# Splitting all first expert weights in the key turns of the walk, two halves a turn, and adding the last skip rows tile by tile

## The reference

```python
xn = _layernorm(x)
# graph attention, summed over the edges of each target node
e = leaky_relu(el[src] + er[dst]); ex = exp(e - emax[dst])
rst = segment_sum(feat[src] * (ex / denom[dst]), dst)
x = x + (xn + elu(rst + bias)) + linear_attention(xn)
# experts: W1 is (8, 256, 1024), W2 is (8, 1024, 256)
h = gelu((layernorm(x) * ln_g + ln_b) @ W1[e] + b1[e])
x = x + sum over the two chosen experts of weight * (h @ W2[e] + b2[e])
```

## Time and profile before

| | us |
|---|---|
| median of 3 runs | 1894.84 (1893.95 to 1897.71) |
| profiled execution, its own time | 1891.82 |
| its span, first to last instruction | 1890.1 |
| start of the walk's first add and end of its last | 119.3 and 1198.4 |
| busy: PE, DVE, POOL, ACT | 1581.7, 1368.5, 1218.3, 1079.1 |
| mean granted TensorE clock | 0.937 of full speed |

### The profile page before, as it was taken

How to read it: one execution, slowest core, us unless ns; L and a number is a source line. 1 busy time by engine, 2 the same in 40 slices (tenths; PEclk the granted TensorE clock), 3 DMA queues, 4 the chain that set the end, 5 groups by cost and what they waited for, 6 DMA issues and landing times. The chain is left out here.

```text
span 1890.1 us, 46784 instructions
## 1 busy us (share of the span) xinstructions
PE 1581.7 (84%) x11358; PEld 1300.0 (69%) x11358; DVE 1368.5 (72%) x3833; ACT 1079.1 (57%) x3043; POOL 1218.3 (64%) x1135
## 2 busy tenths in 40 slices
PE   7858777788787989888887778629999999999995
PEld 5635555455566777777775666517888889888884
DVE  6656567677667888888888999897666656665662
ACT  4655566566666666677666776563444444444441
POOL 2077777777777777777677776105666666666663
PEclk8978899999999999999998888658999999999998
DMA  7745565566544555555555665652333333333332
GB/s 223 247 122 138 168 174 164 165 176 179 150 117 127 155 150 150 141 152 145 142 139 179 183 202 162 200 199 45 53 48 53 49 48 50 53 50 49 46 53 24
DMA packets 149158, 239.37 MB, mean 127 GB/s; under 512 B 27536, under 2 KB 114824, under 8 KB 147624
## 3 DMA queue, kind: packets, MB, share of 16 engines
q0 software_dynamic: 61216, 132.39, 30.4%
q1 hardware_dynamic: 85944, 103.15, 16.8%
q10 hardware_dynamic: 1744, 0.85, 0.2%
HBM read 180.78 MB, written 55.52 MB: 125 GB/s over the span
## 5 line engine op out<-in xcount | busy, mean ns | idle before, releaser
L843 POOL DMA_INDIRECT w_s<-table,w_s x784 | 806.4, 1029 | 279.9 <-issue 231.4
L2092 PE MATMUL bank<-w_s 128*128 128x260 f32 x1952 | 515.9, 410 | 110.3 <-DVE w_s L1536 110.0
L2092 PEld LDWEIGHTS bank<-w_s 128*128 128x128 f32 x1952 | 378.1, 201 | 206.0 <-DVE w_s L1536 139.9
L1026 ACT ACTIVATE w_s<-w_s 128x64 f32 x976 | 260.3, 337 | 68.3 <-ACT w_s L1021 68.1
L1536 DVE SCALAR_TENSOR_TENSOR w_s<-w_s 128x256 f32<-128x256 f32 x732 | 275.7, 426 | 26.7 <-ACT w_s L1026 18.9
L2294 PE MATMUL bank<-acc,w_s 128*128 128x256 f16 (+1 forms) x2736 | 290.4, 265 | 1.6 <-DVE acc L1937 1.5
L2315 PE MATMUL bank<-w_s,acc 128*128 x2520 | 284.5, 273 | 7.2 <-DVE acc L1951 5.5
L907 POOL DMA_INDIRECT out<-mid_g,low_g x105 | 177.2, 1687 | 151.2 <-ACT mid_g L1197 90.6
L2294 PEld LDWEIGHTS bank<-acc,w_s 128*128 x2736 | 252.9, 98 | 30.7 <-issue 2.1
L2315 PEld LDWEIGHTS bank<-w_s,acc 128*128 128x128 f16 x2520 | 245.8, 98 | 37.0 <-issue 8.7
L1033 ACT COPY w_s<-bank 128x512 bf16<-128x512 bf16 x244 | 142.1, 582 | 202.8 <-PE bank L2072 202.3
(11 more groups left out here) (308 smaller groups left out, 2187.6 us busy)
## 6 DMA issues: line engine op xcount, KB each, us to landing
stage<-in_L_ffn_W SPq DMA_DIRECT2D x32, 512.0 KB, 4.2
w_s<-table,w_s POOLq DMA_INDIRECT x784
w_s<-in_x SPq DMA_DIRECT2D x48, 256.0 KB, 4.0
w_s<-xT_d SPq DMA_DIRECT2D x96, 128.0 KB
w_park<-low_g SPq DMA_DIRECT2D x18, 512.0 KB
w_s<-w_park SPq DMA_DIRECT2D x9, 1024.0 KB, 9.1
xn_d<-acc SPq DMA_DIRECT2D x7, 896.0 KB, 5.0
table<-w_s SPq DMA_DIRECT2D x24, 260.0 KB, 3.5
```

What stands on the lines that cost most here:

```text
L843: pool.indirect_dma_start(out=ring[:, u, k, :], out_offset=None, in_=table[:, :], in_offset=bass.IndirectOffsetOnAxis(ap=srcT[:, (q * RING ...
L1026: last = act.activation(m[:, e, 0:GD], rows[:, e, 0:GD], ACT.Copy, scale=m[:, e, GD:HC])
L2092: last = pe.matmul(bank[2 + k.at % 2][:, 0:ROW], hot32[:, k.at % 4, s, :], msg[:, k.at % 2, s, :], start=s == 0, stop=s == SUB - 1)
```

## The change

- All 32 halves, W1's too, are split and parked in the key turns. `PARKS` goes from 18 halves to 16 pairs of halves; the pairs are handled in turns 2 to 17, two halves a turn. Each half has its own space: `stage[:, u]`, and as the place of the result `low_g` for u = 0 and `mid_g` for u = 1. ACT splits the first after step 1 of a turn and the second after step 2, DVE one step later each, as one piece of 1024 columns instead of two of 512. SP no longer waits for a store to land before it issues the next load; ACT waits for it before it overwrites the space.
- The split turns are gone: `SPLIT_TURNS`, `act_split1`, `dve_split1` and SP's W1 loads there. Turns 52 to 60 have no hook, and the late work stays at its steps. SP loads the parked W1 of experts 0 to 4 after the late work of groups 0 to 4, experts 5 and 6 right after the walk and ahead of the W2 loads there, expert 7 as before.
- The load of the first skip rows is now ahead of any weights.
- POOL adds the skip rows of groups 5 and 6 in seven instructions of one tile (256 columns) each instead of one of 1792.

```diff
-PARKS = 2 * (X + 1)
+PARKS = 2 * X
...
+        park_s = [whole[:, :, :].rearrange("p a b -> p (a b)")[:, 0:FF].bitcast(F16).rearrange("p (h f) -> p h f", h=2)
+                  for whole in (low_g, mid_g)]
...
-            def store_half(h):
-                sp.wait_ge(park_low, h + 1)
-                sp.dma_start(w_park[h // 2, :, h % 2], park_s[:, :, :]).then_inc(park_out, 16)
-                sp.wait_ge(park_out, (h + 1) * 16)
+            def store_half(e, u):
+                sp.wait_ge(park_low[u], e + 1)
+                sp.dma_start(w_park[e, :, u], park_s[u][:, :, :]).then_inc(park_out[u], 16)
...
-                h = t // 2 - 3
-                if t % 2 == 0 and 0 <= h < PARKS:
-                    store_half(h)
-                    if h + 1 < PARKS:
-                        load_half(h + 1)
+                e = t // 2 - 3
+                if t % 2 == 0 and 0 <= e < PARKS:
+                    for u in range(2):
+                        store_half(e, u)
+                        if e + 1 < PARKS:
+                            load_half(e + 1, u)
...
+            def load_w1(e):
+                sp.dma_start(w1_s[:, e, :, :, :], w_park[X + e]).then_inc(w1_in, 16)
...
+            load_mid(0)
             for u in range(2):
-                load_w1(0, u)
-            load_mid(0)
-            group_added(0)
-            next_w1(1)
-            next_w1(2)
...
+                sp.wait_ge(park_out[u], 16 * PARKS)
...
+            for g in range(5):
+                group_added(g)
+                load_w1(g)
             sp.wait_ge(msg_ready, J)
             load_mid(GROUPS - 1)
             sp.wait_ge(acc_done, J)
+            load_w1(5)
+            load_w1(6)
             load_w2(1)
...
             def add_mid(g):
-                z = acc[:, g * RG:(g + 1) * RG, 0:D]
...
-                pool.tensor_tensor(z, z, mid_of(g)[:, :, :], ALU.add).then_inc(x2_made, 1)
+                for k in range(RG):
+                    z = acc[:, g * RG + k, 0:D]
+                    last = pool.tensor_tensor(z, z, mid_of(g)[:, k, :], ALU.add)
+                last.then_inc(x2_made, 1)
...
             def park_hook(b, u):
                 keys_hook(b, u)
-                if u == 1:
-                    act.wait_ge(park_in, (b - 1) * 16)
-                    act.activation(park_s[:, 0, :], stage[:, 0, :], ACT.Copy, scale=WSCALE).then_inc(park_high, 1)
+                if u in (1, 2):
+                    e, half = b - 2, u - 1
+                    act.wait_ge(park_in[half], (e + 1) * 16)
+                    if e:
+                        act.wait_ge(park_out[half], e * 16)
+                    act.activation(park_s[half][:, 0, :], stage[:, half, :], ACT.Copy, scale=WSCALE).then_inc(park_high[half], 1)
...
-            def dve_split1(n, u):
...
+            def dve_park(e, half):
+                dve.wait_ge(park_high[half], e + 1)
+                dve.scalar_tensor_tensor(park_s[half][:, 1, :], stage[:, half, :], WSCALE, park_s[half][:, 0, :],
+                                         ALU.mult, ALU.subtract).then_inc(park_low[half], 1)
```

More of the change, by code:

```diff
@@ L123, in past, with walk_turns @@
         return not isinstance(self.n, int) or self.n >= least
-def walk_turns(eng, slot, keys, park, queries, split, end_slot=None, late=None):
+def walk_turns(eng, slot, keys, park, queries, end_slot=None, late=None):
     def turn(b, beside, c):
@@ L145, in walk_turns @@
         turn(q0 + c, queries, c)
-    for n in range(SPLIT_TURNS):
-        turn(s0 + n, split, n)
-    for b in range(s0 + SPLIT_TURNS, end):
+    for b in range(q0 + QUERY_TURNS, end):
         turn(b, None, b)
@@ L508, in build @@
         blank_turn = sem("blank_turn")
-        park_in, park_high, park_low, park_out = sem("park_in"), sem("park_high"), sem("park_low"), sem("park_out")
+        park_in, park_high, park_low, park_out = (
+            [sem(f"{name}{u}") for u in range(2)] for name in ("park_in", "park_high", "park_low", "park_out"))
         w1_in, w2_in, b2_in = sem("w1_in"), sem("w2_in"), sem("b2_in")
-        stage_in = [sem(f"stage_in{u}") for u in range(2)]
-        high_ready = [sem(f"high_ready{u}") for u in range(2)]
-        low_ready = [sem(f"low_ready{u}") for u in range(2)]
         den_turn, scaled, z_exp, elu_made, x2_made = (
@@ L696, in _ @@
                 sp_chunk(c)
-            def load_w1(n, u):
-                sp.dma_start(stage[:, u, :], w1[bass.ds(n, 1), u * P:(u + 1) * P, :].rearrange("e p f -> p (e f)")).then_inc(stage_in[u], 16)
+            def load_w1(e):
+                sp.dma_start(w1_s[:, e, :, :, :], w_park[X + e]).then_inc(w1_in, 16)
             def load_mid(g):
@@ L724, in store_xn2 @@
                              acc[:, g * RG:(g + 1) * RG, 0:D]).then_inc(xn2_out[g % 2], 16)
-            def next_w1(n):
-                for u in range(2):
-                    sp.wait_ge(low_ready[u], n)
-                    load_w1(n, u)
             def group_added(g):
@@ L735, in group_added @@
                 store_x2(g)
+            load_mid(0)
             for u in range(2):
-                load_w1(0, u)
-            load_mid(0)
-            group_added(0)
-            next_w1(1)
-            next_w1(2)
-            group_added(1)
-            next_w1(3)
-            group_added(2)
-            next_w1(4)
-            next_w1(5)
-            group_added(3)
-            next_w1(6)
-            for u in range(2):
-                sp.wait_ge(low_ready[u], X - 1)
+                sp.wait_ge(park_out[u], 16 * PARKS)
             sp.dma_start(b2_b, b2.rearrange("(a e) d -> a e d", a=1).to_broadcast([P, X, D])).then_inc(b2_in, 16)
-            group_added(4)
+            sp.wait_ge(mid_out, 16 * (PAIRS + 1))
+            for g in range(5):
+                group_added(g)
+                load_w1(g)
             sp.wait_ge(msg_ready, J)
@@ L1625, in dve_mid @@
                 last.then_inc(mid_ready, 1)
-            def dve_split1(n, u):
-                dve.wait_ge(high_ready[u], n + 1)
-                dve.scalar_tensor_tensor(w1_half(n, u, 1), stage[:, u, :], WSCALE, w1_half(n, u, 0),
-                                         ALU.mult, ALU.subtract).then_inc(low_ready[u], 1)
-            def dve_park(b, k):
-                dve.wait_ge(park_high, b - 1)
-                half = slice(k * (FF // 2), (k + 1) * (FF // 2))
-                last = dve.scalar_tensor_tensor(park_s[:, 1, half], stage[:, 0, half], WSCALE, park_s[:, 0, half],
-                                                ALU.mult, ALU.subtract)
-                if k == 1:
-                    last.then_inc(park_low, 1)
+            def dve_park(e, half):
+                dve.wait_ge(park_high[half], e + 1)
+                dve.scalar_tensor_tensor(park_s[half][:, 1, :], stage[:, half, :], WSCALE, park_s[half][:, 0, :],
+                                         ALU.mult, ALU.subtract).then_inc(park_low[half], 1)
             def park_hook(b, u):
@@ L1642, in park_hook @@
                 if u >= 2:
[L1643 removed]
+                    dve_park(b - 2, u - 2)
             def keys_hook(b, u):
@@ L2337, in _ @@
             pe_turn_rows(0)
-            for u in range(2):
-                pe.wait_ge(low_ready[u], X - 1)
-            pe.wait_ge(w1_in, 16)
+            pe.wait_ge(w1_in, 16 * X)
             for s in range(FT):
```

34 lines of the change are left out of this document (11 added, 23 removed).

## The result

The changed kernel takes 1902.04 us (median of 7 runs, 1896.06 to 1906.53); the kernel before, beside it, 1896.15 (7 runs, 1893.95 to 1897.71). The ratio is 1.0034, with a 95% interval of 1.0019 to 1.0049: **slower by about 6 us**, where the prediction said 17 us faster.

A forecast was written before the change was run, and what follows sets the result against it. POOL's gathers bound the key turns, DVE the split turns. Terms +3.5 - 13.4 - 3.3 - 2.8 - 1.0 = -17.0 us took the profiled 1891.8 to 1874.8, expected median 1878; 8-in-10 range 1869 to 1890.

The forecast's parts named there:

- What bounds each stage: Key turns 2 to 17: POOL's gathers set the pace; split turns 52 to 58: DVE, busy 125.6 of 130.3 us.
- SP's queue in the key turns: Turns 2 to 17: doubled stores and loads, 54 GB/s on top of 165, cost nothing, hidden by POOL's pace.
- The rival: Key turns: transfers come in one burst, POOL finds rows late; 24 us over 16 turns, 1902 in all; chance 0.06.
- The gathers beside the splits: Turns 2 to 17: DVE splits of 14 more halves lengthen POOL's gathers, +3.5 us (+2.9 to +5.2).
- The rival's 14.4 us: Key turns: splits block gathers for their whole length, costing 14.4 instead of 3.5 us, 1889 in all; chance 0.10.
- The split turns: -13.4: Turns 52 to 58: 17.1 us of DVE splits removed, 3.7 given back as idle time; bounds -15.4 and -5.7.
- The first skip rows: Turn 51: DVE's 4.12 us wait for `mid_g` shrinks as that load goes first, -3.3 us; bounds -2 and -4.1.
- The tile-by-tile adds: Walk's end: DVE waits for one piece of POOL's add at most, -2.8 us; at the second add, -1.0.
- After the walk: Behind the walk: two more parked megabytes, 6.4 us at 330 GB/s, delay nothing wanted before a gap ends; 0.

The follow-up runs named there:

- the splits small: Changed kernel with the splits of every half after the first expert's cut from 1024 to 64 columns, all transfers at full size: 1893.92 us (one run).
- small transfers: Changed kernel with every half after the first expert's cut to 128 columns a row in its loads and stores, splits whole: 1890.05 us (one run).
- both small: Changed kernel with every half after the first expert's cut to 128 columns a row in its transfers and 64 columns in its splits: 1872.73 us (one run).
- staggered halves with two DVE pieces each: Changed kernel with a turn's two halves taken half a turn apart and DVE's split in two 512-column pieces in separate slots: 1877.59 us, ratio 0.9908.

## Why the prediction was wrong

- *What bounds each stage* was right: POOL in the key turns, DVE in the split turns.
- *SP's queue in the key turns: "I price this at nothing; what hides it is the same POOL pace."* **This is the step that failed.** POOL's pace hides nothing from POOL itself, which waits for the rows of its own earlier gathers. I added 54 GB/s to 165 and compared averages, where the change put four transfers of 0.5 MB into 2.5 us and took out the wait that had spaced them. POOL idles 23.2 us more beyond its ordinary gaps, 14.4 of it in waits that the profile names. With the splits small the burst costs 25.1 us; in the changed kernel spacing the same transfers gives back 14.6 to 16.9. The rival had the mechanism and, in part by luck, the price (24 us, 1902): it took one wait of 1.49 us from another stage for every turn, where the long waits were 0.9 to 3.1 us. I gave it a chance of 0.06, because I took the longest wait of before, 0.3 us, for its likelihood, though the pacing behind it was being removed.
- *The gathers beside the splits: +3.5.* Too low as a price of the splits, though the gathers of the changed kernel took only 5.0 us more. In a steady stream it is 17.3 us (small transfers against both small) with two long pieces a turn. I divided the average over all gathers by the number of halves, "near the lower end, since the instructions become one instead of two a half". That is the wrong way round: a piece of 0.68 us caught a gather's start 12 times in 32, one of 1.21 us 31 times in 32, and with more left (0.63 us instead of 0.50). The average without splits that I subtracted was no base either, since message pieces and hit matrices hold gathers up in those turns too. The rule of the Trainium skill that I weighed against the average holds for every gather that starts in a split. The rival's 14.4 us comes near the 14.8 counted by coincidence: it is the growth of DVE's busy time on splits, while the time lost to them grew by 11.1 (4.5 to 15.6), 5.8 of which the other DVE instructions gave back.
- *The split turns: -13.4.* -10.6 in the changed kernel, DVE busy 109.7 (108.5 foretold) and idle 10.0 of 119.7 us, 1.4 a turn instead of 1.2. In the other kernels of the changed form the same turns give -11.2 to -14.8, so the mechanism and size stand.
- *The first skip rows: -3.3.* -3.1, and -3.1 in turn 51 with this part alone.
- *The tile-by-tile adds: -2.8 and -1.0.* Together -3.6 alone. The walk's end gave more (-4.8), in part because DVE's piece came ahead of the add in that profile, and the adds behind it cost 1.2 instead of winning 1.0.
- *After the walk: 0.* +2.1, of which 1.2 are the adds by the run with them alone. Over all profiles of the sets at 1896 us this part takes 690.8 to 694.9 us, so 2 us can be scatter.
- The sum as measured: +1.1 before turn 2 and -2.4 in turns 18 to 50, both of which other runs show as scatter, +28.0, turn 51 -3.1, turns 52 to 58 -10.6, turn 59 -1.2, the walk's last turn -4.6, behind it +2.1: +9.3 us of the 9.4.

The version that the experiments point to, staggered halves with two DVE pieces each, takes 0.9908 of the time before, -17 us. That this is the number promised for the change as it was is a coincidence: its terms are others.

## What to carry over

A wait may cost its own engine nothing and still space out transfers that share the DMA engines with others. Before removing it, count how many bytes can then be in flight at once beside the transfers that the bound engine waits for; averages of bandwidth don't tell. Beside a stream of GpSimd gathers, keep DVE instructions with two SBUF inputs short: what one costs goes by how likely a gather starts in it and how much of it is then left, so two short ones are cheaper than a long one, even back to back. And measure one cost with the other removed: two causes that hide in each other's waits each look small alone.

## What the runs showed that I had not expected

- A gather that starts during a DVE instruction with two SBUF inputs and over 0.13 us before its end ends 0.82 us behind it: in the changed kernel all 30 in a split and all 33 in a message piece or hit matrix. In the kernel before 79 of 89 do so, and of the ten that don't, which took 0.94 or 0.95 us, nine start within 0.03 us of the DVE instruction's own start. In the changed kernel no gather that was already under way was held up.
- DVE's next instruction lets the waiting gather in between (nine of ten), so adjacent pieces are as good as pieces in slots of their own (316.6 and 317.6 us).
- POOL's first add behind the walk starts some 10 us after its last gather in every kernel: 9.99 us idle in the changed one, put down to nothing. The Trainium skill's GPSIMD Engine Reference, the section on instruction dispatch, gives about 6 us for the load of code at the first call to a freshly loaded kernel; no run here took it apart.
- Seven adds of 128x256 on POOL take 5.8 to 6.9 us where one of 128x1792 takes 3.96. Undisturbed pieces follow each other every 0.69 us, which would be 4.8 us for seven, about 0.1 us a piece more. The rest is DVE holding POOL up once more: in the changed kernel one piece of the first seven takes 2.50 us instead of 0.72, since it starts 0.1 us into DVE's scaling of two SBUF inputs (L1659, 2.03 us).
